# A two-layer graph network on one core: output addition one step later, 21 staged chunks, two early scatters for eighteen chunks, and 1 MB node transfers

## The chip, the cores and the metric

One core of one Trainium2 chip runs the whole program. The metric is the device time of one execution in microseconds (us); the median of three executions is compared. TensorE is called PE here, its weight loads PEld, VectorE DVE, ScalarE ACT, GpSimd POOL, and SyncE SP. SP issues nearly all plain DMA transfers, POOL all indirect ones (a row of 512 bytes for each of 128 indices).

## The reference

100000 nodes with 128 features, 50000 edges sorted by destination. A layer of graph attention and a layer of continuous-filter convolution follow each other, each behind a layer norm and a ReLU and with a residual:

```python
h = relu(layernorm(x))
x = x + gat(h, W_l, b_l, W_r, b_r, att, bias, src, dst)   # 4 heads, a self loop on every node
h = relu(layernorm(x))
x = x + filters(h, edge_attr_20, edge_weight, dst, src, W_in2f, Wf1, bf1, Wf2, bf2, Wo1, bo1, Wo2, bo2)

# gat:      m = leaky_relu(x_l[s] + x_r[d]);  e = m . att;  alpha = softmax of e over the edges of a destination
#           out[d] = sum of alpha * x_l[s] + bias
# filters:  msg = (h @ W_in2f)[src] * Wij(edge_attr) * edge_weight;  agg[dst] = sum of msg
#           out = ssp(agg @ Wo1 + bo1) @ Wo2 + bo2          # ssp(z) = softplus(z) - log 2
```

Here the convolution gathers at `idx_j = dst` and sums at `idx_i = src`.

## The kernel before

The work runs in four stages, one after the other on the same core. Nodes are handled in 49 groups of 2048 rows (1 MB), edges in 98 chunks of 512 (4 tiles of 128).

**Stage 1, dense nodes (to about 487 us).** A node with no edge attends only to itself, so its row is x + relu(norm(x)) W_l + bias. For each of the 49 groups SP loads x into one of four buffers `d_x` (`load`, L359) and stores the result from one of two buffers `d_x1` (`store`, L380), each in four transfers of 256 KB, a quarter of every partition's 8 KB row at a time (2 KB). The load of group g+4 is issued right behind the store of group g. DVE makes the statistics (`sums_d`, L877) and adds the residual in quarters (`x1_d`, L885); ACT normalises; PE transposes and multiplies (`step_d` on each engine). Beside the first four groups DVE prepares weights and edge lists (`beside`, L932) and PE turns the lists (`turn_lists`, `turn_last_list`). Meanwhile POOL gathers edge rows ahead (list `ahead`, L687): 18 **staged** chunks, which it writes on to DRAM (`store_stage`, L679) because there are only 24 slots for chunks, and then the first 18 chunks, which stay. Each entry of the list waits until a number of quarters of groups is done (`done`, L690).

**Stage 2, attention (to about 1434 us).** Fully unrolled over 98 chunks plus a lag: in step t the front of chunk t (scores) and the back of chunk c = t - 12 (shares, scan, output) run on the engines, in an order written out by hand (`step_a` on each engine). DVE's step is: difference `a_dif` (L1048); after ACT has copied the values, `a_u` (L1061); gate, product and scan of chunk c (L1067 to L1075); statistics of chunk t+4 (`sums_a`); in even steps the shift of a norm (`shifts`, L772), for which ACT waits before it normalises `a_ns` (L1294) and then makes `a_us` (L1347) and `a_xs` (L1349); then the output addition of chunk c into `a_xo` (L1096), which waits for PE's transposed product of the same step (L1609, `out_turned`); in odd steps the variances. Every seven chunks a pack of small row operations lies between. Once `a_xo` is there, SP stores the chunk (L447) and POOL writes its first tile of result rows into the node array (`early_scatters`, L659; the other three tiles wait for stage 3). POOL gathers the remaining 56 chunks, spread over the first 80 steps (L706 to L713); SP loads a staged chunk back when its slot is free (L451). In step t SP first issues the loads of shares and gates for chunk t - 11 (L439, L440), then waits for the addition of chunk t - 13 and stores it.

**Stage 3, convolution (to about 2637 us).** Chunks run in reverse order (97 first), so that a running sum carries over chunk borders. For each chunk POOL writes the three late tiles of the attention result (`scatters`, L718, L724) and adds the 4 tiles of messages of two chunks before into the sums in DRAM (`adds`, L728, L736); before the first add it waits until the additions of the previous chunk have landed.

**Stage 4, output network (to the end).** Over the 49 groups: load sums, load x1, compute, store, all in transfers of 1 MB with 8 KB a partition.

Of the kernel before, what the change touches and what calls it, by code (L numbers as in the profile page):

```python
# [34 lines left out]
TILES = 4  # L35
# [21 lines left out]
STAGED = 18  # L57
# [15 lines left out]
def gnn(nc, x, src, dst, edge_attr, edge_weight, W_l, b_l, W_r, b_r, att, bias,  # L73
# [27 lines left out]
    with ExitStack() as ctx:  # L101
# [239 lines left out]
        def late(s):  # L341

            return 16 * (TILES - EARLY[1 - s])
# [10 lines left out]
        def _(sp):  # L354
# [35 lines left out]
            for g in range(ROUNDS * RX, NG):  # L390
                if g == NG - 1:

                    sp.wait_ge(x1_stored[(g - 1) % RN], 16 * QUADS * in_slot[(g - 1) % RN])
                store(g, g % RX)
                if g + RX < NG:
                    load(g + RX, g % RX)
# [66 lines left out]
            for i in range(RN):  # L463
                sp.wait_ge(x1_stored[i], 16 * QUADS * in_slot[i])
                sp.sem_inc(sync_step, 1)
# [7 lines left out]
            for s in range(2):  # L473
                sp.wait_ge(end_stored[s], 16 * HALF)
                sp.wait_ge(early_scattered[s], 16 * EARLY[s] * HALF)
# [3 lines left out]
            def load_rows_b(k, u, t0):  # L479
# [12 lines left out]
                if t0 >= 2:  # L492
                    sp.wait_ge(x1_scattered[s], late(s) * turn(k, u - 2))
                    sp.sem_inc(sync_step, 1)
# [7 lines left out]
            def step_b(k, u, t0, ahead=True):  # L502
# [3 lines left out]
                if ahead:  # L506
                    load_rows_b(k, u + 1, t0 + 1)
# [11 lines left out]
            load_rows_b(0, 0, 0)  # L519
            for u in range(4):  # L520
                step_b(0, u, u)
            with sp.Fori(2, HALF - 1) as k:
# [6 lines left out]
            for s in range(2):  # L529
                sp.wait_ge(x1_scattered[s], late(s) * HALF)  # L530
# [38 lines left out]
        def _(pool):  # L569
# [89 lines left out]
            def early_scatters(t):  # L659
                s = t % 2  # L660
                pool.wait_ge(x1_ready, t + 1)
                if t >= 2:
                    pool.wait_ge(early_scattered[s], 16 * EARLY[s] * (t // 2))
                pool.sem_inc(pool_step, 1)
                for j in range(EARLY[s]):
# [23 lines left out]
            for n, (gather, t, h) in enumerate(ahead):  # L689
                done = QUADS * (RX + 1) + n * QUADS * (NG - RX - 3) // len(ahead)  # L690
# [5 lines left out]
            for i in range(RN):  # L696
                pool.wait_ge(x1_stored[i], 16 * QUADS * in_slot[i])
# [20 lines left out]
            def scatters(k, u):  # L718
# [4 lines left out]
                for j in range(EARLY[1 - s], TILES):  # L723
# [15 lines left out]
            for u in range(4):  # L739
                scatters(0, u)  # L740
                if u >= 2:
                    adds(0, u - 2, first=u == 2)
            with pool.Fori(2, HALF) as k:
                for u in range(2):
                    scatters(k, u)
# [32 lines left out]
        def _(dve):  # L778
# [98 lines left out]
            def sums_d(g, slot, m, half):  # L877
                if half == 0:
                    dve.wait_ge(xd_loaded[slot], 16 * QUADS * (m + 1))
# [5 lines left out]
            def x1_d(g, slot, m, q):  # L885

                dve.wait_ge(d_mm, QUADS * g + q + 1)
                if q == 0 and not (isinstance(g, int) and g < RN):
                    dve.wait_ge(x1_stored[slot % RN], 16 * QUADS * (RX // RN * m + slot // RN))
# [42 lines left out]
            beside = (output_bias, edge_lists, edge_weights, index_columns)  # L932
# [103 lines left out]
            def step_a(t):  # L1036
# [26 lines left out]
                if back:  # L1063
                    s = c % 2
                    dve.wait_ge(spread[s], 64 * (c // 2 + 1))
                    dve.wait_ge(keep_loaded[s], 16 * (c // 2 + 1))
                    dve.scalar_tensor_tensor(out=a_gate[:, :], in0=a_beta[s][:, :], scalar=-1.0, in1=a_keep[s][:, :],  # L1067
# [3 lines left out]
                    if c >= 1:  # L1071
                        dve.wait_ge(sum_scan, c)
# [18 lines left out]
                if back:  # L1091
                    dve.wait_ge(out_turned, c + 1)
                    if c >= 4:
                        dve.wait_ge(end_stored[s], 16 * ((c - 4) // 2 + 1))
                        dve.wait_ge(early_scattered[s], 16 * EARLY[s] * ((c - 4) // 2 + 1))
                    dve.tensor_tensor(a_xo[c % 4][:, :], bank[6 + c % 2][:, :], a_xd[c % DEPTH][:, :], ALU.add).then_inc(x1_ready, 1)  # L1096
# [9 lines left out]
            for i in range(RN):  # L1106
                dve.wait_ge(x1_stored[i], 16 * QUADS * in_slot[i])
            for t in range(NC + LAG):
# [3 lines left out]
            for s in range(2):  # L1112
                dve.wait_ge(end_stored[s], 16 * HALF)
                dve.wait_ge(early_scattered[s], 16 * EARLY[s] * HALF)
# [142 lines left out]
        def _(act):  # L1257
# [112 lines left out]
            for i in range(RN):  # L1370
                act.wait_ge(x1_stored[i], 16 * QUADS * in_slot[i])
# [16 lines left out]
            def norms_b(k, u, t0):  # L1388
# [4 lines left out]
                if t0 >= 2:  # L1393
                    act.wait_ge(x1_scattered[s], late(s) * turn(k, u - 2))
# [9 lines left out]
            def step_b(k, u, t0, ahead=True, front=True, mid=True, back=True):  # L1404
# [30 lines left out]
                if ahead:  # L1435
                    norms_b(k, u + 1, t0 + 1)
# [3 lines left out]
            norms_b(0, 0, 0)  # L1440
            for u in range(4):
                step_b(0, u, u, mid=u >= 1, back=u >= 2)
            with act.Fori(2, HALF - 1) as k:
# [34 lines left out]
        def _(pe):  # L1478
# [59 lines left out]
            for g in range(RX):  # L1538
                step_d(g, g, back=g > 0)
                if g == 0:  # L1540
                    output_bias()
                if g == 2:
                    turn_lists()
            turn_last_list()
# [199 lines left out]
```

## Time and profile before

| what | us |
|---|---|
| median of 3 runs (lowest, highest) | 3022.98 (3020.04, 3025.41) |
| the profiled execution, its own time | 3014.57 |
| its span, first to last instruction | 3012.7 |
| PE, DVE, ACT, POOL busy | 2392.7, 2267.1, 1939.7, 1908.9 |

The profiled execution is 8.4 us below the median of the other runs. A window row gives the busy time of each engine in a stretch, with the number of instructions in brackets, the granted TensorE clock, the busy share of the 16 DMA engines and the GB/s that they moved. A timeline row is one instruction (or a few of one kind merged) with its start and length in us; in brackets at its end stands how long its engine was idle before it and what ended that. A row of waits gives a line, what released it, the total of the idle time in us, how often, and the longest. "issue" is idle time in which the engine waited for nothing that the profile shows.

### The profile page before, as it was taken

The page shows a single profiled execution, that of the slowest core. Times are in us where ns is not written, and L with a number is a line of the kernel's source. Part 1 is how long each engine was busy: PE and PEld are TensorE (multiplying, and loading weights), DVE is VectorE, ACT ScalarE, POOL GpSimd, SP SyncE. Part 2 cuts the span into 40 slices and gives each one's busy share as a digit, 9 for nine tenths or more (in the row PEclk, how much of TensorE's full clock was granted, in tenths as well). Part 3 has the DMA queues.
Part 4 walks back from the last instruction along what each step waited for, and adds up shares of the span by engine and source line. Part 5 has one row for each costly group of instructions (what it writes and reads, how often), then busy time and mean ns, then how long its engine had stood idle before and what let it go on. Part 6 is the DMA issues. An engine that isn't in the chain of part 4 may idle for free. (4 is left out here: it accounts for less than half of the span.)

```text
span 3012.7 us, 59625 instructions
## 1 busy us (share of the span) xinstructions
PE 2392.7 (79%) x16506; PEld 1659.0 (55%) x16506; DVE 2267.1 (75%) x6293; ACT 1939.7 (64%) x4383; POOL 1908.9 (63%) x1650
## 2 busy tenths in 40 slices
PE   5888997998899998997677777777777777488777
PEld 4666664344444444445555555555555555377777
DVE  7777875688888878876787777777787787366666
ACT  5878886766666666660555555555555555289887
POOL 2677776377777777742588888888888888600000
PEclk9999998999999999996899899999899899789998
DMA  7999995266566655554566666666655656689998
GB/s 224 299 310 326 287 292 189 84 192 188 179 211 191 192 189 188 179 171 130 113 117 119 111 117 113 119 113 117 119 112 115 124 113 123 173 322 425 426 426 338
DMA packets 390076, 593.04 MB, mean 197 GB/s; under 512 B 148151, under 2 KB 225323, under 8 KB 364818
## 3 DMA queue, kind: packets, MB, share of 16 engines
q1 hardware_dynamic: 291682, 479.21, 48.4%
q0 software_dynamic: 98288, 112.65, 19.0%
q8 instruction: 39, 0.64, 0.1%
q14 instruction: 67, 0.55, 0.1%
HBM read 353.86 MB, written 246.47 MB: 199 GB/s over the span
## 5 line engine op out<-in xcount | busy, mean ns | idle before, releaser
L736 POOL DMA_INDIRECT sum_dram<-b_sum,b_at x392 | 636.9, 1625 | 148.5 <-issue 119.4
L650 POOL DMA_INDIRECT a_xs<-in_x,index x320 | 331.5, 1036 | 108.1 <-issue 98.9
L657 POOL DMA_INDIRECT a_xd<-in_x,index x320 | 328.7, 1027 | 97.5 <-issue 87.5
L724 POOL DMA_INDIRECT x_dram<-b_xo,sidx x294 | 312.7, 1064 | 105.1 <-issue 90.6
L1666 PE MATMUL bank<-b_rows,b_same 128*128 128x128 bf16 x4704 | 307.5, 231 | 0.6 <-ACT b_sum L1434 0.6
L1666 PEld LDWEIGHTS bank<-b_rows,b_same 128*128 128x128 bf16 x4704 | 292.6, 104 | 0.6 <-issue 0.6
L1275 ACT ACTIVATE d_n<-d_x,stat_d_shift,stat_d_rstd 128x128 f32<-128x128 f32 x686 | 283.5, 486 | 0.2 <-DVE stat_d_shift L772 0.2
L1699 PE MATMUL bank<-wo,f_ssp_out 128*128 128x128 f32 x1568 | 228.1, 292 | 63.1 <-DVE f_ssp_out L1221 61.5
L1699 PEld LDWEIGHTS bank<-wo,f_ssp_out 128*128 128x128 f32 x1568 | 204.4, 203 | 80.1 <-DVE f_ssp_out L1221 73.8
L1481 PE MATMUL bank<-ident,d_n 128*128 128x128 f32 x1184 | 193.2, 289 | 67.3 <-DMA d_n<-sum_dram 38.0
L1527 PE MATMUL bank<-wl,turned 128*128 128x128 f32 x1568 | 234.9, 295 | 10.8 <-ACT turned L1272 9.5
L1527 PEld LDWEIGHTS bank<-wl,turned 128*128 128x128 f32 x1568 | 196.8, 197 | 58.9 <-issue 35.7
L881 DVE BATCH_NORM_STATS2 stat_d_six<-d_x 128x6 f32<-128x128 f32 x784 | 160.4, 278 | 79.2 <-DMA d_x<-in_x 79.2
L666 POOL DMA_INDIRECT x_dram<-a_xo,index x98 | 117.6, 1200 | 155.6 <-DVE a_xo L1096 131.2
L1646 PEld LDWEIGHTS bank<-wo,b_msg 128*128 128x128 f32 x784 | 116.5, 226 | 169.5 <-issue 90.7
L1646 PE MATMUL bank<-wo,b_msg 128*128 128x128 f32 x784 | 134.1, 324 | 81.2 <-DVE b_msg L1162 80.8
L1061 DVE SCALAR_TENSOR_TENSOR a_u<-bank,cols,a_xs 128x512 f32<-128x512 f32 x98 | 73.6, 751 | 160.7 <-ACT a_xs L1349 160.7
L1235 DVE TENSOR_TENSOR d_x<-bank,d_x 128x512 f32<-128x512 f32 x180 | 123.0, 685 | 89.4 <-DMA out<-d_x 87.9
L1481 PEld LDWEIGHTS bank<-ident,d_n 128*128 128x128 f32 x1184 | 142.8, 148 | 84.7 <-DMA d_n<-sum_dram 38.1
L1294 ACT ACTIVATE a_ns<-a_xs,stat_e_shift,stat_e_rstd 128x128 f32<-128x128 f32 x392 | 160.7, 480 | 43.5 <-DVE stat_e_shift L772 43.5
L1424 ACT ACTIVATE b_rows<-bank 128x512 bf16<-128x512 f32 x98 | 58.4, 595 | 201.0 <-PE bank L1646 200.8
L1221 DVE SCALAR_TENSOR_TENSOR f_ssp_out<-bank,cols,f_ln_out 128x512 f32<-128x512 f32 x196 | 146.3, 746 | 53.8 <-ACT f_ln_out L1466 53.4
(234 smaller groups left out, 6138.8 us busy)
## 6 DMA issues: line engine op xcount, KB each, us to landing
d_x<-in_x SPq DMA_DIRECT2D x196, 256.0 KB
x_dram<-d_x SPq DMA_DIRECT2D x196, 256.0 KB
out<-d_x SPq DMA_DIRECT2D x49, 1024.0 KB, 10.1
sum_dram<-zero SPq DMA_DIRECT2D x48, 1024.0 KB
d_x<-x_dram SPq DMA_DIRECT2D x45, 1024.0 KB, 14.2
d_n<-sum_dram SPq DMA_DIRECT2D x25, 1024.0 KB, 11.9
a_beta<-beta_dram SPq DMA_DIRECT2D x392, 64.0 KB
x_end_dram<-a_xo SPq DMA_DIRECT2D x98, 256.0 KB, 3.0
```

Of the source, the lines that this page charges most:

```text
L650: pool.indirect_dma_start(a_xs[t % DEPTH][:, j * F:(j + 1) * F], None, x, column(t, j)).then_inc(gathered[t % GSEM], 16)
L657: pool.indirect_dma_start(a_xd[t % DEPTH][:, j * F:(j + 1) * F], None, x, column(t, TILES + j)).then_inc(gathered[t % GSEM], 16)
L724: pool.indirect_dma_start(x1_dram, bass.IndirectOffsetOnAxis(ap=sidx[s][:, j:j + 1], axis=0), b_xo[s][:, j * F:(j + 1) * F], None, bounds_ ...
L736: pool.indirect_dma_start(sum_dram, bass.IndirectOffsetOnAxis(ap=b_at[s][:, j:j + 1], axis=0), b_sum[s][:, j * F:(j + 1) * F], None, compu ...
L881: last = dve.bn_stats(stat_d[slot % 2]["six"][:, j, :], d_x[slot][:, j * F:(j + 1) * F])
L1275: last = act.activation(d_n[slot % RN][:, j * F:(j + 1) * F], d_x[slot][:, j * F:(j + 1) * F], ACT.Relu, scale=stat_d[slot % 2]["rstd"][:, ...
L1294: return act.activation(to[:, j * F:(j + 1) * F], rows[:, j * F:(j + 1) * F], ACT.Relu, scale=st["rstd"][:, n:n + 1], bias=st["shift"][:, ...
L1481: last = pe.transpose(to[0:width, j * P:(j + 1) * P], tiles[:, j * width:(j + 1) * width], ident[:, :])
L1527: last = pe.matmul(to[:, j * F:(j + 1) * F], turned[q % 2][:, j * P:(j + 1) * P], wl[:, :], start=False, stop=(j == 3))
L1646: last = pe.matmul(bank[5][:, j * F:(j + 1) * F], b_msg[:, j * P:(j + 1) * P], wo1[:, :], start=True, stop=True)
L1666: last = pe.matmul(bank[6][:, i * F:(i + 1) * F], b_same[s][:, j, i * P:(i + 1) * P], b_rows[s][:, part, j * F:(j + 1) * F], start=(j == 0 ...
L1699: last = pe.matmul(bank[4 + q][:, j * F:(j + 1) * F], f_ssp_out[q][:, j * P:(j + 1) * P], wo2[:, :], start=True, stop=True)
```

## The change

1. In stage 2 the output addition of chunk c moves from the end of DVE's step c + 12 into the next step, behind that step's scan and ahead of the statistics and the shift; there is one more step at the end. The gate's wait for the scan before moves ahead by two instructions.
2. 21 instead of 18 chunks are staged. The gathers ahead in stage 1 begin after group 3 instead of group 5; for that the index columns are made in the third group and the weights in the fourth, and PE turns the lists one group earlier.
3. For the last 18 chunks (80 to 97) two tiles instead of one are scattered early in stage 2, and two instead of three in stage 3, where these chunks come first. The loops of stage 3 on SP, ACT and POOL are split in two for it.
4. Each load and store of a node group in stage 1 is one transfer of 1 MB instead of four of 256 KB.

```diff
-STAGED = 18
+STAGED = 21
+LAST = 18
+RUNS = 1
+LAST_EARLY = 2
...
+        def early_of(c):
+            return LAST_EARLY if c >= NC - LAST else EARLY[c % 2]
...
             def load(g, slot):
-                for q in range(QUADS):
-                    sp.dma_start(d_x[slot][:, q * 512:(q + 1) * 512], node_rows(x, g)[:, q * 512:(q + 1) * 512]).then_inc(xd_loaded[slot], 16)
+                sp.dma_start(d_x[slot][:, :], node_rows(x, g)).then_inc(xd_loaded[slot], 16)
...
             def store(g, slot):
                 sp.wait_ge(d_x1_ready, QUADS * g + QUADS)
-                for q in range(QUADS):
-                    sp.dma_start(node_rows(x1_dram, g)[:, q * 512:(q + 1) * 512],
-                                 d_x1[slot % RN][:, q * 512:(q + 1) * 512]).then_inc(x1_stored[slot % RN], 16)
+                sp.dma_start(node_rows(x1_dram, g), d_x1[slot % RN][:, :]).then_inc(x1_stored[slot % RN], 16)
...
-                for j in range(EARLY[s]):
+                for j in range(early_of(t)):
                     pool.indirect_dma_start(x1_dram, column(t, 2 * TILES + j), a_xo[t % 4][:, j * F:(j + 1) * F], None,
...
-                done = QUADS * (RX + 1) + n * QUADS * (NG - RX - 3) // len(ahead)
+                done = QUADS * (RX - 1) + n * QUADS * (NG - RX - 1) // len(ahead)
...
-                for j in range(EARLY[1 - s], TILES):
+                for j in range(EARLY[1 - s] if later else LAST_EARLY, TILES):
                     pool.indirect_dma_start(x1_dram, bass.IndirectOffsetOnAxis(ap=sidx[s][:, j:j + 1], axis=0),
...
-            beside = (output_bias, edge_lists, edge_weights, index_columns)
+            beside = (output_bias, edge_lists, index_columns, edge_weights)
...
+                    if c >= 1:
+                        dve.wait_ge(sum_scan, c)
                     dve.scalar_tensor_tensor(out=a_gate[:, :], in0=a_beta[s][:, :], scalar=-1.0, in1=a_keep[s][:, :],
...
                     dve.tensor_tensor_scan(a_o[s][:, :], a_gate[:, :], a_pv[:, :], a_o[1 - s][:, C - 1:C] if c else 0.0,
                                            ALU.mult, ALU.add).then_inc(sum_scan, 1)
+                c = t - LAG - 1
+                if 0 <= c < NC:
+                    s = c % 2
+                    dve.wait_ge(out_turned, c + 1)
+                    if c >= 4:
+                        dve.wait_ge(end_stored[s], 16 * ((c - 4) // 2 + 1))
+                        dve.wait_ge(early_scattered[s], 16 * early_upto(c - 4))
+                    dve.tensor_tensor(a_xo[c % 4][:, :], bank[6 + s][:, :], a_xd[c % DEPTH][:, :], ALU.add).then_inc(x1_ready, 1)
...
-                if back:
-                    dve.wait_ge(out_turned, c + 1)
...
-                    dve.tensor_tensor(a_xo[c % 4][:, :], bank[6 + c % 2][:, :], a_xd[c % DEPTH][:, :], ALU.add).then_inc(x1_ready, 1)
...
-            for t in range(NC + LAG):
+            for t in range(NC + LAG + 1):
                 step_a(t)
```

## Rows read from the trace of the kernel before

**Rows 1.** Windows, three stages: length, busy by engine, clock, DMA share, GB/s

```profile
75.00:150.00 75.00, 66.66 (x438) 49.12 (x437) 58.32 (x233) 65.39 (x169) 49.80 (x55) 1.00 0.93 298
1700.00:1900.00 200.00, 143.83 (x1395) 112.99 (x1393) 154.73 (x414) 113.08 (x252) 161.50 (x118) 0.92 0.63 116
2700.00:2900.00 200.00, 159.50 (x1296) 152.70 (x1296) 137.97 (x215) 178.51 (x324) 0.00 (x0) 0.96 1.01 425
```

**Rows 2.** Waits of DVE, 80 to 470 us: line, releaser, total us, times, longest

```profile
DVE stat_d_six L881 <- DMA d_x<-in_x: 67.7, 37, 4.2
```

**Rows 3.** Timeline of DVE, first stage: start, us, engine, line, operation, idle before

```profile
82.28 0.18 DVE L772 SCALAR_TENSOR_TENSOR stat_d_shift<-stat_d_sum,stat_d_rstd 128x16 f32<-128x16 f32 x1 [0.30 <-ACT stat_d_rstd L768]
341.54 0.17 DVE L772 SCALAR_TENSOR_TENSOR stat_d_shift<-stat_d_sum,stat_d_rstd 128x16 f32<-128x16 f32 x1
349.78 0.18 DVE L772 SCALAR_TENSOR_TENSOR stat_d_shift<-stat_d_sum,stat_d_rstd 128x16 f32<-128x16 f32 x1
455.11 0.17 DVE L772 SCALAR_TENSOR_TENSOR stat_d_shift<-stat_d_sum,stat_d_rstd 128x16 f32<-128x16 f32 x1
```

**Rows 4.** Windows with 2 KB packets alone, and with gathers alone

```profile
65.00:85.00 20.00, 17.80 (x113) 13.83 (x113) 16.79 (x68) 17.75 (x46) 0.39 (x1) 0.91 0.70 218
505.00:540.00 35.00, 30.88 (x99) 11.71 (x98) 19.04 (x76) 26.45 (x66) 26.47 (x29) 1.00 0.18 54
```

**Rows 5.** POOL: first and last gather of stage 1, its longest wait after

```profile
84.61 1.05 POOL L675 DMA_INDIRECT a_xs<-in_x,index  x1 [39.36 <-issue]
472.70 0.94 POOL L657 DMA_INDIRECT a_xd<-in_x,index  x1 [0.30 <-issue]
POOL x_dram L666 <- DVE a_xo L1096: 41.6, 1, 41.6
```

**Rows 6.** Waits of ACT, 600 to 1280 us

```profile
ACT a_ns L1294 <- DVE stat_e_shift L772: 39.0, 37, 1.4
```

**Rows 7.** Timeline of odd steps of the second stage, DVE and ACT

```profile
603.23 0.67 ACT L1347 ACTIVATE a_us<-bank,cols 128x512 f32<-128x512 f32 x1
604.05 0.60 ACT L1349 ACTIVATE a_xs<-bank 128x512 f32<-128x512 f32 x1 [0.16 <-PE bank L1586]
1283.68 0.16 DVE L772 SCALAR_TENSOR_TENSOR stat_e_shift<-stat_e_sum,stat_e_rstd 128x16 f32<-128x16 f32 x1
1283.76 0.68 DVE L1096 TENSOR_TENSOR a_xo<-bank,a_xd 128x512 f32<-128x512 f32 x1
1283.87 1.65 ACT L1294 ACTIVATE a_ns<-a_xs,stat_e_shift,stat_e_rstd 128x128 f32<-128x128 f32 x4 [1.23 <-DVE stat_e_shift L772]
1285.74 0.69 ACT L1347 ACTIVATE a_us<-bank,cols 128x512 f32<-128x512 f32 x1 [0.22 <-PE bank L1584]
1286.60 0.60 ACT L1349 ACTIVATE a_xs<-bank 128x512 f32<-128x512 f32 x1 [0.17 <-PE bank L1586]
```

**Rows 8.** End of stage 2: a wait of DVE; timeline, SP and DVE

```profile
DVE a_xo L1096 <- PE bank L1609: 21.0, 14, 2.2
1392.96 0.42 SPq L440 DMA_DIRECT2D a_keep<-gate_dram  x1
1396.05 0.69 DVE L1067 SCALAR_TENSOR_TENSOR a_gate<-a_beta,a_keep 128x512 f32<-128x512 f32 x1 [1.23 <-DMA a_keep<-gate_dram]
```

**Rows 9.** Stage 3: groups of the page, waits of POOL, DVE timeline

```profile
L736 POOL DMA_INDIRECT sum_dram<-b_sum,b_at x392 | 636.9, 1625 | 148.5 <-issue 119.4
L724 POOL DMA_INDIRECT x_dram<-b_xo,sidx x294 | 312.7, 1064 | 105.1 <-issue 90.6
POOL sum_dram L736 <- DMA sum_dram<-b_sum,b_at: 10.1, 7, 1.8
POOL x_dram L724 <- DMA sum_dram<-b_sum,b_at: 6.1, 20, 0.3
1459.16 0.69 DVE L1126 TENSOR_TENSOR b_y<-b_x,bo_row 128x512 f32<-128x512 f32 x1
1468.30 0.69 DVE L1126 TENSOR_TENSOR b_y<-b_x,bo_row 128x512 f32<-128x512 f32 x1
```

More of the change, by code:

```diff
@@ L339, in early, with early_upto, scattered_b @@
             return EARLY[s] * F
-        def late(s):
-            return 16 * (TILES - EARLY[1 - s])
+        def early_of(c):
+            return LAST_EARLY if c >= NC - LAST else EARLY[c % 2]
+        def early_upto(c):
+            return sum(early_of(i) for i in range(c % 2, c + 1, 2))
+        def scattered_b(k, u, later):
+            s = u % 2
+            few = 16 * (TILES - LAST_EARLY)
+            many = 16 * (TILES - EARLY[1 - s])
+            if not later:
+                return few * turn(k, u)
+            return many * turn(k, u) - (many - few) * (LAST // 2)
         def node_rows(a, g):
@@ L492, in load_rows_b @@
                 if t0 >= 2:
-                    sp.wait_ge(x1_scattered[s], late(s) * turn(k, u - 2))
+                    sp.wait_ge(x1_scattered[s], scattered_b(k, u - 2, later))
                     sp.sem_inc(sync_step, 1)
@@ L517, in step_b @@
                 sp.dma_start(b_col[s][:, :], columns[:, bass.ds(8 * (NC - 1 - t), 8)]).then_inc(b_col_ld[s], 16)
-            load_rows_b(0, 0, 0)
+            load_rows_b(0, 0, 0, later=False)
             for u in range(4):
-                step_b(0, u, u)
-            with sp.Fori(2, HALF - 1) as k:
+                step_b(0, u, u, later=False)
+            with sp.Fori(2, LAST // 2) as k:
+                for u in range(2):
+                    step_b(k, u, 4 + u, later=False)
+            step_b(LAST // 2, 0, 4, later=False)
+            step_b(LAST // 2, 1, 5)
+            with sp.Fori(LAST // 2 + 1, HALF - 1) as k:
                 for u in range(2):
@@ L716, in _, with scatters @@
             pool.wait_ge(cleared, 16 * NG)
-            def scatters(k, u):
+            def scatters(k, u, later):
                 s = u % 2
@@ L739, in _ @@
             for u in range(4):
-                scatters(0, u)
+                scatters(0, u, False)
                 if u >= 2:
                     adds(0, u - 2, first=u == 2)
-            with pool.Fori(2, HALF) as k:
+            with pool.Fori(2, LAST // 2) as k:
                 for u in range(2):
-                    scatters(k, u)
+                    scatters(k, u, False)
+                    adds(k, u - 2)
+            with pool.Fori(LAST // 2, HALF) as k:
+                for u in range(2):
+                    scatters(k, u, True)
                     adds(k, u - 2)
@@ L1393, in norms_b @@
                 if t0 >= 2:
-                    act.wait_ge(x1_scattered[s], late(s) * turn(k, u - 2))
+                    act.wait_ge(x1_scattered[s], scattered_b(k, u - 2, later))
                 act.activation(b_xo[s][:, early(1 - s):], b_x[s][:, early(1 - s):], ACT.Copy).then_inc(b_xo_ready, 1)
@@ L1435, in step_b @@
                 if ahead:
-                    norms_b(k, u + 1, t0 + 1)
+                    norms_b(k, u + 1, t0 + 1, later)
             act.wait_ge(ones_set, 1)
             inverse_deviation(act, stat_e[0], TILES, b_var, b_logv, b_rstd, 1)
-            norms_b(0, 0, 0)
+            norms_b(0, 0, 0, later=False)
             for u in range(4):
-                step_b(0, u, u, mid=u >= 1, back=u >= 2)
-            with act.Fori(2, HALF - 1) as k:
+                step_b(0, u, u, mid=u >= 1, back=u >= 2, later=False)
+            with act.Fori(2, LAST // 2) as k:
+                for u in range(2):
+                    step_b(k, u, 4 + u, later=False)
+            step_b(LAST // 2, 0, 4, later=False)
+            step_b(LAST // 2, 1, 5)
+            with act.Fori(LAST // 2 + 1, HALF - 1) as k:
                 for u in range(2):
```

42 lines of the change are left out of this document (19 added, 23 removed).

## The prediction

> **What bounds the kernel now.** The four stages follow each other, so I read each by itself: first the windows, then the waits of each stage, then single steps in the timeline. The chain that ended last is of little use here: it begins at 2584 us and covers stage 4, which the change leaves alone.
>
> In stage 1 the DMA engines are busy for 0.93 of the time at 298 GB/s, while ACT and PE stand at 65 to 67 of 75 us [rows 1]. DVE waits 67.7 us in 37 of about 43 groups for the load of x [rows 2]. From one shift to the same shift of the next group is 8.24 us in an undisturbed pair; over 42 groups, 82.28 to 455.11, the mean is 8.88 us [rows 3]. So the engines could do 8.24 and the loads make it 8.88. Does that bandwidth explain it? Before the gathers start, 2 KB packets alone move 218 GB/s at a share of 0.70, so 311 GB/s at full share or 105 ns a packet and engine; gathers alone make 54 GB/s at 0.18, 300 GB/s or 27 ns for a row of 512 B [rows 4]. A group is 1024 packets of 2 KB (1024 x 0.105 / 16 = 6.72 us), its part of the 36 staged stores (36 x 128 x 0.105 / 16 / 42 = 0.72) and 288 / 42 = 6.9 gathers (6.9 x 128 x 0.027 / 16 = 1.49): 8.9 us, just the mean period. Stage 1 is bound by DMA.
>
> Stage 2 is a round trip between DVE, ACT and PE, read below in single steps. In stage 3 POOL is busy 161.5 of 200 us [rows 1], and with the gap of some 0.3 us behind every indirect transfer it is full: four adds at (636.9 + 148.5) / 392 = 2.0 us and three scatters at (312.7 + 105.1) / 294 = 1.4 us [rows 9] are 12.3 us a chunk, start of the stage included. Its other engines can do better: while POOL does not yet hold them, two chunks follow each other in 9.14 us [rows 9].
>
> **1 MB transfers (stage 1).** The bytes stay; 256 packets of 8 KB replace 1024 of 2 KB in a group, and SP issues one DMA where it issued four. No row shows 8 KB packets in stage 1; the nearest is stage 4, which moves 1 MB transfers at 425 GB/s and share 1.01 [rows 1], 311 ns for 8 KB. A group's 256 packets then take 256 x 0.311 / 16 = 4.98 us instead of 6.72. The staged stores and gathers of the change (42 and 312) add 0.84 + 1.5. The sum is 7.3 us, under 8.24: ACT's chain becomes the bound, and 42 x (8.88 - 8.24) = **27 us** fall away. The bounds are 7.3 us (nothing left to wait for) and the present price of a byte, 6.72 + 2.34 = 9.06 us, which would cost 42 x 0.18 = 8 us. I take the row of stage 4, because its transfers have the very shape; the two prices meet the 8.24 us at 5.9 us for 2 MB, 355 GB/s. Nothing waits for a quarter today (every wait counts all four), so larger transfers hold nobody up.
>
> The Trainium skill (DMA: Bandwidth & Descriptors, "Why small descriptors are slow (HBM only)") speaks against this: a packet costs its 32-byte beats and about three cycles more. By that, 64 + 3 against 256 + 3 beats, bytes would get only 3.4% cheaper, the group would take 8.8 us, and stage 1 would gain some 3 us. The rows at 311 and 425 GB/s say 27% instead, though of different stages; it stays a rival.
>
> **Three more staged chunks.** 24 gathers and 6 stores move from stage 2 into stage 1. There POOL is busy from 84.61 to 473.6 [rows 5], about 1.25 us a gather without a pause; it grows by 24 x 1.25 + 6 x 0.6 = 34 us and begins some 17 us sooner (two groups), so it ends near 490, after the dense groups, which then end near 455. That costs nothing: POOL goes straight on to its six resident chunks (48 x 1.25 = 60 us; today it has to wait for the last stores first), is through some 6 us later than now, and now waits 41.6 us there for the first addition of stage 2 [rows 5]. That addition comes 27 us sooner by stage 1 and 8 us later by its own step: 41.6 - 6 - 27 + 8 = 17 us of slack are left. In stage 2, 24 gathers less help nobody: DVE never waits there for a gather. If that cover were gone, each chunk late by x would cost x.
>
> **The addition one step later (stage 2).** DVE has the same instructions in every step, and in steady steps it did not wait for PE's product, because the statistics lay between. Moving the addition saves nothing there. But in even steps it passes the shift: scan, addition, statistics, shift. The shift comes an addition later, 0.68 less the 0.08 by which neighbours overlap, 0.60 us, while the next `a_dif` stays in place. ACT already waits for that shift 39.0 us in 37 steps [rows 6], and then runs `a_ns` 1.65, `a_us`, `a_xs`, for which DVE's `a_u` waits. The slack is 0.22 + 0.17 us in a plain odd step and 0.16 in one with pack work [rows 7], so `a_xs` is late by 0.21 or 0.44. Of the 40 odd steps from 15 to 93, 23 are in pack phases 1 to 4: 23 x 0.44 + 17 x 0.21 = **+13.7 us**. Bounds: 0, were PE late anyway, and 40 x 0.60 = 24.
>
> At the end, where statistics run out, DVE does wait for PE: 21.0 us in 14 steps [rows 8]. This goes, but not in full. SP is moved too: it now waits for an addition that comes after the next chunk's scan before it issues the next loads of shares and gates. From that addition to a usable gate are about 0.5 us for the store, 1.75 for four loads and 3.1 for the gate (issued 1392.96, used 1396.05 [rows 8]), 5.4 us, and then gate, product, scan and addition, 3.2 us: 8.6 us for two steps, 4.3 a step, against 4.5 to 5.4 now. Followed chunk by chunk the tail ends **6.5 us** sooner; bounds 0 and 14. POOL's second early scatter behind the last chunk adds **1.3 us**. The other 17 fall into waits of POOL and are covered. Stage 2: +8.5 us in sum.
>
> **Two early scatters (stage 3).** 18 scatters of 1.4 us leave POOL, but the first three chunks fill the pipeline and POOL idles there; 15 count. The new wait: adds of a chunk wait until the last adds have landed, today hidden behind three scatters. In 20 chunks the landing fell into the gap just before a scatter, in 7 it came after all three and cost 1.4 us each [rows 9]. So it usually takes two to four us, three scatters cover 4.1, two cover 2.7. I take 0.4 us of new wait, 1.36 - 0.4 = 0.96 for each of 15, **14 us** gained. Bounds: 0.35 each (all land late, 5 us) and 1.36 (20 us). The other engines' 9.14 us stay below POOL's 11.
>
> **Sum.** -27 + 13.7 - 6.5 + 1.3 - 14 = -33 us. Against the profiled execution's own 3014.6 that is 2982; against the median of 3022.98, 8.4 us higher, **2990 us**.
>
> **The rivals.** (a) *A byte keeps its price in stage 1.* Then stage 1 runs at 8.8 to 9.06 us a group, -3 to +8 us, by the rule above or by plain queueing of loads and stores. For it: the two prices come from different stages. Against it: stage 4 is also full of mixed loads and stores. With the rest (+8.5 - 14) it gives 3014 to 3026. (b) *Slower*, the same mechanism with the new wait of stage 3 at its bound: the extra gathers and stores make stage 1 DMA-bound at 9.06 (+8), the late shift costs 13.7 - 5, and the adds land late (-5): 3023 + 8 + 8.7 - 5 = 3035. It decides where 2 MB take more than 6.6 us beside the gathers. (c) *The late shift costs the full 0.60* in every odd step and the tail gains nothing, because PE's turning and SP's loads hold it: +24 instead of +7, 3007. (d) *POOL sets the pace*, so that fewer gathers speed up stage 2: its gaps there are all near 0.3 us, and 24 x 1.25 = 30 us more would go, 2960. Against it: DVE waits for ACT, not for gathers. (e) *The change does not do what it says*, the shorter first stage being eaten by POOL's longer list: 2990 + 27 = 3017.
>
> **How the numbers follow.** Forecast 0.66; (a) 0.11; (b) 0.06; (c) 0.09; (d) 0.04; (e) 0.04. The forecast's own range is 2972 to 3004, from its bounds. The range 2965 to 3014 takes in (c) and the near end of (a). What a measurement can tell from no change is about 0.2%, 6 us. Faster: forecast, (c), (d), a part of (e) and half of (a), 0.86; same: the rest of (a) and (e), 0.07; slower: (b) and what little of (c) costs more, 0.07.
>
> **What would show it.** Right: a period of 8.2 to 8.3 us in stage 1, hardly any wait for x, and a DMA share near 0.85 there; ACT's wait for the shift up by 20 to 25 us; the tail's steps at 4.3 us with DVE waiting for gates instead of PE; POOL in the first 18 chunks of stage 3 at 10.5 to 11 us with short waits on the adds. Wrong: a share still at 0.93 and periods of 8.8; an unchanged wait for the shift; a stage 2 that shrinks by more than 10 us; scatters and adds at 12 us a chunk from the first on.

## The result, and the profile after

The changed kernel takes **2997.46 us** in the median of its runs (2997.24 to 2999.34), against 3022.98 before: a ratio of 0.9924, 95% interval 0.9902 to 0.9946, or 25.5 us less (16 to 30 by the interval). The forecast was 2990 us with a range of 2965 to 3014. The profiled execution took 2997.2 us (span 2995.3), 17.4 us less span than the profiled execution of before; that one happened to be 8 us under its own median, so the traces account for 17 of the 25 us.

Reading the same instructions in both timelines divides these 17.4 us: the first difference of stage 2 (`a_dif` of chunk 0) starts at 456.6 instead of 492.2 (-35.6); the way from there to the last addition takes 964.2 instead of 937.5 us (+26.7); from there to the first add of stage 3 nothing changes; stage 3 from its first add to the start of the last four is 1149.7 instead of 1161.8 (-12.0); the rest +3.6, which is scatter (below). So stage 1 gave more than forecast, and stage 2 took most of it away.

The windows of after (length, busy time by engine, clock, DMA share, GB/s), stages 1 and 4, to be read against [rows 1]:

```profile
75.00:150.00 75.00, 71.28 (x469) 52.83 (x468) 63.05 (x254) 69.51 (x181) 58.58 (x66) 1.00 0.96 340
150.00:225.00 75.00, 71.81 (x471) 53.13 (x471) 63.79 (x256) 70.05 (x182) 59.06 (x67) 1.00 0.97 350
...
2700.00:2900.00 200.00, 158.55 (x1288) 151.53 (x1287) 139.52 (x216) 178.53 (x323) 0.00 (x0) 0.96 1.01 426
```

In stage 1 PE and ACT are now busy 71 and 70 of 75 us, and DMA moves 340 to 350 GB/s. But its share did not fall to 0.85: it is still 0.96 to 0.97. The waits of DVE in stage 1 (80 to 455 us), against [rows 2]:

```profile
DVE d_x L911 <- PE bank L1555: 25.4, 52, 1.4
DVE stat_d_shift L793 <- ACT stat_d_rstd L789: 24.9, 38, 0.7
DVE stat_d_six L902 <- DMA d_x<-in_x: 7.9, 14, 1.5
```

The wait for x fell from 67.7 us to 7.9. In its place DVE waits for PE and ACT, so the engines set the pace. Two shifts 41 periods apart, against [rows 3]:

```profile
79.47 0.18 DVE L793 SCALAR_TENSOR_TENSOR stat_d_shift<-stat_d_sum,stat_d_rstd 128x16 f32<-128x16 f32 x1 [0.20 <-ACT stat_d_rstd L789]
419.50 0.18 DVE L793 SCALAR_TENSOR_TENSOR stat_d_shift<-stat_d_sum,stat_d_rstd 128x16 f32<-128x16 f32 x1 [0.74 <-ACT stat_d_rstd L789]
```

(419.50 - 79.47) / 41 = 8.29 us a group: ACT's 8.24 with little on top.

Stage 2: the waits of ACT from 600 to 1280 us, against [rows 6]; the wait of DVE for gathered rows near the end of the stage (1160 to 1305 us); and its wait for gates in the tail (1344 to 1425 us):

```profile
ACT a_ns L1317 <- DVE stat_e_shift L793: 51.8, 37, 3.2
...
DVE stat_e_six L978 <- DMA a_xd<-in_x,index: 11.1, 3, 8.2
...
DVE a_gate L1090 <- DMA a_keep<-gate_dram: 17.9, 5, 5.4
```

The first line is the late shift (39.0 us before): 12.8 us more, where the prediction looked for 20 to 25. Also behind the addition now is the row work of the packs on DVE, for which ACT waits 54.1 us in this stretch (rows `p_dec`, `p_run`, `p_exp`, `p_col`), 29.0 before. The third shows the tail as forecast in kind: DVE waits for SP's loads, where it waited for PE ([rows 8]). The second is something that the prediction does not have. Before, DVE waited 0.3 us in all for gathers near the end of the stage; now one step of 9.5 us becomes one of 17.9. The timeline of DVE and POOL around that step:

```profile
1285.71 0.67 DVE L1105 TENSOR_TENSOR a_xo<-bank,a_xd 128x512 f32<-128x512 f32 x1
1286.29 0.66 DVE L996 TENSOR_REDUCE p_col<-p_tail 32x1 f32<-32x513 f32 x1
1295.15 0.87 DVE L978 BATCH_NORM_STATS2 stat_e_six<-a_xs 128x6 f32<-128x128 f32 x4 [8.20 <-DMA a_xd<-in_x,index]
...
1260.22 1.01 POOL L683 DMA_INDIRECT x_dram<-a_xo,index  x1 [3.77 <-DVE a_xo L1105]
...
1287.32 1.02 POOL L683 DMA_INDIRECT x_dram<-a_xo,index  x1 [0.77 <-issue]
1288.64 0.97 POOL L674 DMA_INDIRECT a_xd<-in_x,index  x1 [0.30 <-issue]
1289.92 0.95 POOL L674 DMA_INDIRECT a_xd<-in_x,index  x1 [0.31 <-issue]
```

DVE has nothing to do from 1286.95 to 1295.15. The two gathers of `a_xd` at 1288.64 and 1289.92, whose rows then land, stand in POOL's order behind the early scatter at 1287.32. That scatter sends the sum of the addition that is now a step later; at 1260.22 POOL stood still 3.77 us for another such addition, with all later gathers behind it. POOL's list spreads the gathers over the scatters of the first 80 chunks, not over the first 80 steps; the scatter at 1287.32 is that of chunk 78, which DVE adds in step 91 now, the long step, and added in step 90 before. POOL's waits for additions, from 700 us to the last gathers, before (to 1323 us) and after (to 1306 us):

```profile
POOL x_dram L666 <- DVE a_xo L1096: 1.1, 1, 1.1
...
POOL x_dram L683 <- DVE a_xo L1105: 47.8, 14, 10.0
```

So POOL is not short of time in the changed kernel, which has 24 gathers fewer here: before, it ran behind the additions and hardly ever waited for one; now it stands still for 47.8 us, with gathers that DVE will need behind the wait.

Stage 3: the groups of the page (busy us, mean ns, idle before), against [rows 9]:

```profile
L753 POOL DMA_INDIRECT sum_dram<-b_sum,b_at x392 | 639.6, 1632 | 155.0 <-issue 108.7
L741 POOL DMA_INDIRECT x_dram<-b_xo,sidx x276 | 292.7, 1060 | 102.3 <-issue 87.4
```

and POOL's wait for the adds to land in the first sixteen chunks (1460 to 1640 us):

```profile
POOL sum_dram L753 <- DMA sum_dram<-b_sum,b_at: 12.7, 10, 1.7
```

Eighteen scatters have left L741. The sixteen periods from the first add of a chunk to that of the next take 11.3 us in the mean, 12.0 before (forecast: 10.5 to 11); further on both kernels have 11.96.

### The profile page after: what moved, and what is told of

Same layout as the page of the kernel before. It is cut to its first block, busy times and chain, and to the rows that moved or that the text cites. A ratio compares the mean times of both kernels' runs of the same rounds, so it can differ in the third digit from the quotient of the medians.

```text
span 2995.3 us, 58792 instructions
## 1 busy us (share of the span) xinstructions
PE 2392.2 (80%) x16506; PEld 1653.3 (55%) x16506; DVE 2264.1 (76%) x6293; ACT 1932.7 (65%) x4383; POOL 1903.8 (64%) x1656
## 4 chain that ended last, share of the span: by engine, by line
DMA 18%; issue 9%; POOL 8%; DVE 6%; PE 4%; SPq 3%; ACT 2%; POOLq 0%; DVEq 0%; ACTq 0%
DMA out<-d_x 7%; POOL sum_dram L753 5%; DMA b_end<-ends 4%; DMA sum_dram<-b_sum,b_at 3%; POOL x_dram L741 3%; DMA x_dram<-b_xo,sidx 2%; PE bank L1695 2%; DVE d_x L1258 1%; DMA b_w<-weight_dram 1%; DVE stat_e_six L1152 1%; DVE f_ssp_out L1244 1%; PE bank L1675 1%; DVE b_y L1149 1%; ACT f_exp_out L1488 1%; DVE b_s L1190 1%
## 5 line engine op out<-in xcount | busy, mean ns | idle before, releaser
L674 POOL DMA_INDIRECT a_xd<-in_x,index x308 | 316.7, 1028 | 93.9 <-issue 92.6
L667 POOL DMA_INDIRECT a_xs<-in_x,index x308 | 312.4, 1014 | 93.9 <-issue 91.7
L741 POOL DMA_INDIRECT x_dram<-b_xo,sidx x276 | 292.7, 1060 | 102.3 <-issue 87.4
L683 POOL DMA_INDIRECT x_dram<-a_xo,index x116 | 134.7, 1162 | 165.0 <-DVE a_xo L1105 125.4
L1174 DVE TENSOR_TENSOR_SCAN b_fill<-b_goes,b_fill,bank 128x512 f32<-128x512 bf16 x97 | 124.0, 1278 | 76.3 <-DMA b_goes<-goes_dram 75.7
L1483 ACT ACTIVATE f_abs_out<-bank,cols 128x512 f32<-128x512 f32 x196 | 136.9, 698 | 60.3 <-PE bank L1509 59.9
## 6 DMA issues: line engine op xcount, KB each, us to landing
d_x<-x_dram SPq DMA_DIRECT2D x45, 1024.0 KB, 14.2
```

Of the source, the lines that this page charges most:

```text
L667: pool.indirect_dma_start(a_xs[t % DEPTH][:, j * F:(j + 1) * F], None, x, column(t, j)).then_inc(gathered[t % GSEM], 16)
L674: pool.indirect_dma_start(a_xd[t % DEPTH][:, j * F:(j + 1) * F], None, x, column(t, TILES + j)).then_inc(gathered[t % GSEM], 16)
L741: pool.indirect_dma_start(x1_dram, bass.IndirectOffsetOnAxis(ap=sidx[s][:, j:j + 1], axis=0), b_xo[s][:, j * F:(j + 1) * F], None, bounds_ ...
```

## The experiments

All were timed beside the kernel before. Ratios are to that kernel; the changed one stands at 0.9924. This table gives stretches of each profiled execution in us, read as above: start of `a_dif` of chunk 0; from there to that of chunk 84; on to that of chunk 97, the last; on to the last addition (the tail); on to the first add of stage 3; its first 16 chunks; the others to the start of the last four adds; and to the end.

```
kernel             first a_dif  to 84  to 97  tail  to add  16 ch.  others  end
before                   492.2  745.5  118.4  73.7    36.9   192.3   969.4  384.4
after                    456.6  755.2  132.3  76.7    36.8   180.8   969.0  388.0
e1 add_back              460.1  746.9  118.1  75.1    38.6   181.9   973.4  380.5
e2 gathers_sooner        456.7  755.9  119.2  73.5    37.6   180.6   968.7  382.8
e3 quarters              491.9  755.6  132.6  74.1    38.3   182.4   967.5  384.2
e4 one_early             459.1  755.7  132.3  73.9    37.7   190.0   971.0  381.0
e5 staged18              456.8  757.9  126.2  74.1    39.5   182.1   970.9  384.9
e6 behind_shift          457.4  852.0  134.4  75.0    38.3   182.3   972.1  387.2
e7 behind_store          456.6  857.2  137.7  62.0    37.7   181.8   974.8  381.2
e8 last30                457.1  858.4  137.3  62.7    39.8   181.2   962.3  383.5
e9 hybrid                457.4  748.2  117.7  62.9    39.1   183.1   971.8  382.1
e10 hybrid_last30        457.1  746.1  132.7  63.9    40.1   178.8   965.5  380.7
e11 hybrid_staged18      456.0  744.8  119.6  63.6    39.4   181.2   965.8  380.4
e12 only_1mb             460.9  747.1  123.0  74.9    38.0   191.5   968.3  391.0
```

The last column has the same instructions in all kernels and lies between 380.4 and 391.0: the 3.6 us above are of that kind.

**e1: the addition back in its place.** The block goes back behind the shift, with the chunk of its own step (`c = t - LAG`):

```diff
-                c = t - LAG - 1
-                if 0 <= c < NC:
...
                     shifts(dve, stat_e[pair % 2], 4 * TILES, rstd, shift, pair + 1)
+                if back:
+                    dve.wait_ge(out_turned, c + 1)
...
-            for t in range(NC + LAG + 1):
+            for t in range(NC + LAG):
```

> The changed kernel with the addition back behind the shift of its own step; transfers, staged chunks and scatters stay changed. Theory: the later addition cost stage 2 all that it lost, 9.8 us up to step 84 (the shift that comes after it in even steps), 13.9 us in steps 85 to 92 (the gathers that POOL issues behind the scatter of this addition come a step later, and DVE waits for them) and 3 us in the tail. Undone, the time is 2997 - 24 = 2973 us (2967 to 2982), ACT's wait for the shift is back near 39 us, and no step near the end of the stage is 18 us long. Rival: stage 2 lost its time to the gathers that the three staged chunks and the shorter stage 1 pushed into it; then the long steps 85 to 92 stay, only the 9.8 us come back, and the time is 2985 to 2990 us. Rival two: the tail needs the later addition; then the tail takes 6 us more and the time is 2979 to 2983.

Measured: 2974.75 us, 0.9845 (0.9825 to 0.9865): 0.8% or 24 us faster than with the later addition. ACT's wait for the shift, 600 to 1280 us, is that of before:

```profile
ACT a_ns L1315 <- DVE stat_e_shift L793: 38.5, 37, 1.4
```

The steps up to 84 take 8.3 us less, those from 84 to 97 14.2. The late addition alone made stage 2 slower, and without it the change gives twice as much. The long steps that the first rival would have kept are gone: step 91 takes 9.6 us.

**e2: gathers a step sooner.** Addition as in the changed kernel; in POOL's loop:

```diff
-                until = min(len(rest), -(-len(rest) * (t + 1) // (NC - LAG - 6)))
+                until = min(len(rest), -(-len(rest) * (t + 2) // (NC - LAG - 6)))
```

> The changed kernel, but POOL issues behind the scatter of chunk t the gathers that stood behind that of chunk t+1, so that the gathers come when they came before the change. Theory: the 13.9 us lost in steps 85 to 92 are waits of DVE for gathers that stand in POOL's order behind the scatter of an addition that comes a step later; with the gathers a step sooner the wait of DVE for a_xd near the end (11.1 us in 3 steps) is gone, the time is 2997 - 13 = 2984 us (2980 to 2988), and the wait for the shift stays at 47 us. Rival: POOL is full there, so the gathers cannot come sooner; the wait stays and the time is 2995 to 2999. Rival two: the sooner gathers wait for buffers that are not free and hold up the scatters behind them; slower, 3000 to 3010.

Measured: 2981.39 us, 0.9877 (0.9855 to 0.9900). The waits of DVE from 1160 to 1290 us hold no gathers any more:

```profile
DVE a_u L1082 <- ACT a_xs L1372: 20.9, 13, 2.3
DVE a_u L1082 <- issue: 2.5, 1, 2.5
```

The stretch from 84 to 97 falls from 132.3 to 119.2; the tail is 3.2 us shorter, and all else up to the last adds stays within 1 us. POOL had room; the gathers merely stood behind the wrong scatter.

**e3: the node rows in quarters again.**

```diff
-                sp.dma_start(d_x[slot][:, :], node_rows(x, g)).then_inc(xd_loaded[slot], 16)
+                for q in range(RUNS):
+                    sp.dma_start(d_x[slot][:, q * 512:(q + 1) * 512], node_rows(x, g)[:, q * 512:(q + 1) * 512]).then_inc(xd_loaded[slot], 16)
```

and the stores in the same way, with `RUNS = 4`.

> The changed kernel with the node rows of stage 1 in four transfers of 256 KB again, loads and stores both. Theory: 2 KB packets cost more time for a byte than 8 KB packets in this stage too; the period goes from 8.3 back to 8.9 to 9.1 us, DVE waits 60 us or more for x again, and the time is 2997 + 30 = 3027 us (3021 to 3036). Rival: stage 1 became shorter because the gathers start some 20 us sooner and are spread otherwise, not by the size of the transfers; then the period stays at 8.3 to 8.5 and the time at 2997 to 3004.

Measured: 3031.26 us, 1.0043 (1.0028 to 1.0058), 1.2% or 36 us more than the changed kernel. Its groups take 9.0 us in the mean. A window of stage 1:

```profile
150.00:225.00 75.00, 66.64 (x435) 48.92 (x435) 56.79 (x228) 65.96 (x169) 58.79 (x67) 1.00 0.98 326
```

and DVE's wait for x (80 to 455 us):

```profile
DVE stat_d_six L905 <- DMA d_x<-in_x: 66.8, 37, 4.4
```

The wait is back (66.8 us), and so is the first `a_dif` at 491.9. At nearly the same share the DMA engines move 326 GB/s here and 350 in the changed kernel, of the same mix of rows, staged stores and gathers.

**e12: 1 MB transfers alone**, put into the kernel before (the edit of e3 the other way round).

> The kernel before with nothing but the 1 MB transfers of the node rows in stage 1, loads and stores. Theory: they alone bring the period from 9.0 to 8.3 us and end stage 1 some 34 us sooner; stage 2 has no later addition, so all of it stays: 3023 - 34 = 2989 us, 0.989 (0.9865 to 0.9905). Rival: a part of the shorter stage 1 came from the gathers' earlier start (20 us sooner); then the gathers end later, stage 2 waits for the first ones, and the gain is 20 us or less: 0.9935 to 0.996.

Measured: 2994.12 us, 0.9910 (0.9892 to 0.9928), just beyond the first range (0.9905), which lies in the interval. The first `a_dif` comes at 460.9, 31 us sooner than before and 4 later than in the changed kernel; the steps from 84 to 97 take 4.6 us more than before, for which DVE waits 3.4 us for gathers. So the transfers do nearly all of stage 1; alone they are worth as much as the whole change.

**e4: one early scatter.** `LAST_EARLY = 1`, loops still split.

> The changed kernel with one early scatter in the last eighteen chunks, as in all others; the loops of stage 3 stay split. Theory: the eighteen scatters go back to stage 3, where POOL is full; sixteen chunks there take 12.0 us instead of 11.3, stage 3 is 11.5 us longer, stage 2 ends 1 us sooner at most, and the time is 2997 + 11 = 3008 us (3004 to 3013). Rival: with two early scatters the tail of stage 2 is held up by POOL as much as stage 3 gains; then 2997 to 3002. Rival two: the wait for the landing of the adds costs less than it seems; then 2997 + 18 = 3015.

Measured: 3002.65 us, 0.9949 (0.9931 to 0.9967), 7.5 us more than the changed kernel; the intervals overlap. The trace is plainer: 190.0 instead of 180.8 us for sixteen chunks, and a tail (73.9) like that of e2 with two (73.5). POOL's wait for the adds to land there (1469 to 1660 us):

```profile
POOL sum_dram L753 <- DMA sum_dram<-b_sum,b_at: 0.7, 1, 0.7
```

against 12.7 us in 10 with two early scatters: the new wait exists, and it eats a part of what the scatter saves. The 9.2 us of the traces lie between the theory (11) and the first rival (none); its held-up tail is not seen.

**e5: 18 staged chunks.** `STAGED = 18`.

> The changed kernel with 18 staged chunks instead of 21; POOL gathers 24 rows' columns more in stage 2. Against the kernel before, the changed kernel stands at 0.9924. Theory: POOL has room in stage 2 (it waits 73 us there for additions), so the staged chunks bring nothing; stage 1 gives the same 8.3 us period, the stretch to step 84 stays at 755 us, the long steps 85 to 92 stay or grow by 1 to 3 us: 0.992 to 0.994. Rival: the three chunks are what gives POOL its room; without them the gathers are late in the whole stage and the time is 15 to 30 us more, 0.997 to 1.002. Rival two: stage 1 is eased by 24 gathers and 6 stores less, -5 us, 0.9905.

Measured: 2993.68 us, 0.9906 (0.9885 to 0.9927), within the uncertainty of the changed kernel. The ratio is that of the second rival, but not by its way: stage 1 is the same to 0.2 us. The late gathers still cost DVE, a little less than with 21 (126.2 us from step 84 to 97, not 132.3), and why less stays open; e11 repeats this without them.

**e6: the addition a step later, but behind the shift**, with the gathers of e2. The block of `a_xo` moves from behind the scan:

```diff
-                c = t - LAG - 1
-                if 0 <= c < NC:
...
                     shifts(dve, stat_e[pair % 2], 4 * TILES, rstd, shift, pair + 1)
+                c = t - LAG - 1
+                if 0 <= c < NC:
```

> The changed kernel with the gathers a step sooner, and with the addition still a step later than before, but behind the shift in its step instead of ahead of it. Theory: the 9.8 us lost up to step 84 are the late shift; with the addition behind it they come back in full, ACT's wait for the shift is near 39 us again, the tail is that of the later addition, and the time is 9 us under that of the kernel with sooner gathers alone (0.9877 of the kernel before): 0.9847. Rival: the 9.8 us are the price of a fuller step of DVE, not of the shift; then nothing changes, 0.9877. Rival two: additions later in the step make scatters, and the gathers behind them, later again; steps near the end grow and the time is 0.988 to 0.992.

Measured: 3100.61 us, 1.0248 (1.0224 to 1.0271), some 125 us more than the theory gave, by something that none of the three theories had. A wait of PE from 600 to 1200 us:

```profile
PE bank L1604 <- DVE a_xo L1119: 99.3, 56, 3.7
```

and two rows of the timeline:

```profile
717.40 0.67 DVE L1119 TENSOR_TENSOR a_xo<-bank,a_xd 128x512 f32<-128x512 f32 x1
718.13 0.39 PE L1604 MATMUL bank<-bias_d,ones 3*128 3x512 bf16 x1 [1.64 <-DVE a_xo L1119]
```

PE opens each step with the base of a chunk's output (L1604), in one of two banks, and waits for the addition that empties it. With the addition a step later, this is the one that DVE makes in the step just gone; at the end of that step it comes too late, and PE's whole next step, behind which ACT and DVE wait, starts after it. In e2, with the addition right behind the scan, PE's waits in the same stretch don't contain it. So of the two places that were tried for the later addition, early in the step makes the shift pay, and late makes PE pay. The 9.8 us of the theory can't be read from this run.

**e7 and e8: on top of e6.** e7 lets SP store a sum a step later, so that its loads don't stand behind that wait; e8 alone has two early scatters in the last 30 chunks as well.

```diff
-                c = t - LAG - 1
+                c = t - LAG - 2
...
-LAST = 18
+LAST = 30
```

> As the kernel with the addition behind the shift and sooner gathers, and SP waits for an addition, to store it, a step later than there, so the loads of shares and gates no longer stand behind that wait. Theory: in the tail the gates' loads set the pace of 4.6 us a chunk; with them issued earlier the seven chunks behind the last shares go at 3.3 to 3.6 us, the tail is 66 to 68 us instead of 73.5, and the time is 6 us under its sister: 0.9827. Rival: the loads also wait until the product of two chunks earlier has left their buffer, and the tail stays within 1 us: 0.9847. Rival two: the later store of a chunk's rows holds up the additions four chunks on; slower by 3 to 8 us, 0.986 to 0.987.

> As the kernel with the later store, and two early scatters in the last thirty chunks instead of eighteen. Theory: twelve more chunks of stage 3 go at 11.3 us instead of 12.0, 8.4 us less, and the twelve scatters of 1.3 us fall into waits of POOL in stage 2, which has some 60 us of them: 8 us under its sister, 0.980. Rival: POOL is full where these chunks are gathered (steps 80 to 92), the gathers come late again and eat 8 us or more: 0.9827 to 0.987.

Measured: 3087.33 us, 1.0209 (1.0186 to 1.0232), and 3080.73 us, 1.0190 (1.0166 to 1.0213). Both inherit PE's wait. Against e6 the tail of e7 is 62.0 instead of 75.0 us: the loads did set its pace. Against e7, e8 gains 12.5 us in the later chunks of stage 3, 8.6 of them in the twelve that the edit changes (136.2 us instead of 144.8; forecast 8.4); the rest is scatter, and its ratio is not separable.

**e9: each place where it is cheap.** The old place up to step 93, none in step 94, then a step later behind the scan; SP's store as in e7. The first block stands behind the scan, the second, for `c = t - LAG`, behind the shift:

```diff
+                c = t - LAG - 1
+                if t > NC - LEAD and 0 <= c < NC:
...
+                if back and t < NC - LEAD:
```

> The changed kernel with the addition in its old place, behind the shift of its own step, up to step 93, none in step 94, and from step 95 a step later, right behind the scan; SP waits for an addition, to store it, a step later than now. Theory: the steady steps cost what they did before the change (747 us to step 84, 82 us from there to 93), PE finds its bank free, and the tail, where DVE waited for PE, gets the later addition with gates loaded earlier: 66 to 69 us instead of 75.1 in the kernel with the addition back. Against the kernel before, that kernel stood at 0.9845; this one 7 us lower: 0.982. Rival: the tail is set by the shares of the last pack, 33 us behind the last difference, and by the way from there; then the tail is within 2 us of 75 and the ratio is 0.984 to 0.985. Rival two: the switch costs a bank, PE waits for the addition in steps 95 to 97 and the tail grows: 0.986.

Measured: **2964.12 us, 0.9811** (0.9789 to 0.9833), faster than the kernel before and the changed one. The steps cost what they did before, and the tail is 62.9 us. DVE's wait for gates in it (1323 to 1386 us) went from 17.9 us to

```profile
DVE a_gate L1090 <- DMA a_keep<-gate_dram: 5.2, 4, 3.5
```

SP's later store without the later addition was not run. In the tail of e1 (1325 to 1401 us) DVE waits 1.3 us for gates and 21.1 us for PE's product, so there the loads have little to give: it takes both edits.

**e10: e9 with two early scatters in thirty chunks.**

> The hybrid kernel (addition in its old place up to step 93, later in the tail, SP's store a step later), and two early scatters in the last thirty chunks instead of eighteen. Theory: twelve more chunks of stage 3 at 11.3 instead of 12.0 us, their scatters fall into waits of POOL in stage 2 (57 us with the addition back): 8 us under its sister, 0.9795. Rival: POOL's order delays the gathers again near steps 80 to 92, and half or more is lost: 0.981 to 0.985.

Measured: 2966.91 us, 0.9826 (0.9806 to 0.9847): no gain over e9. Stage 3 is 10.6 us shorter (9.4 in the twelve chunks that the edit changes), and steps 84 to 97 are 15.0 us longer, by the wait that the changed kernel has (DVE, 1160 to 1305 us):

```profile
DVE stat_e_six L978 <- DMA a_xd<-in_x,index: 12.8, 3, 7.0
```

Here the addition is in its old place; twelve scatters more, some 1.3 us each, ahead of the last gathers suffice. POOL's order near the end of stage 2 has hardly any slack, whatever uses it up.

**e11: e9 with 18 staged chunks.**

> The hybrid kernel with two early scatters in the last eighteen chunks, and 18 staged chunks instead of 21. Without the late gathers of the changed kernel in the way, this shows what the three staged chunks are worth. Theory: nothing; POOL has the room for 24 gathers more in stage 2, stage 1 stays at 8.3 us a group because ACT sets it, steps up to 84 take 748 us and those from 84 to 93 take 82: 0.981, within 0.002. Rival: POOL becomes too full with 30 us of gathers more, DVE waits for them near steps 84 to 93, and 5 to 15 us are lost: 0.983 to 0.986. Rival two: stage 1 starts sooner or runs faster with fewer gathers: 0.9795 or less.

Measured: 2961.65 us, 0.9815 (0.9800 to 0.9829), the same as e9: three more staged chunks are worth nothing that can be measured.

## Why the prediction was right, and where its steps failed

**Stage 1 (forecast -27, measured -35.6; e3 gives 36).** The mechanism was right: loads too slow by packet size, ACT next in line (PE is as busy, but waits for ACT's `d_n` 13.5 us in 40, and ACT for PE 4.2 us in 6, 80 to 455 us). Two sizes were off. First a counting error: the shifts at 82.28 and 455.11 [rows 3] are 41 periods apart, not 42, so the mean was 9.09 us, not 8.88; 41 x (9.09 - 8.29) = 33 us, and the shorter first groups add the other 3. Second, the price of a packet: 311 ns for 8 KB was the price of stage 4, and a group was to need 7.3 us (7.4, as 312 gathers come to 1.6 us by the same formula, not 1.5). The trace has 340 / 0.96 = 354 and 350 / 0.97 = 361 GB/s at full share, where e3 has 326 / 0.98 = 333: the mix got 6 to 8% cheaper, not 18%. A group then needs 0.97 x 8.29 = 8.0 us, only just under ACT's 8.24. That the size came out so well is luck in part, because ACT's floor cut the gain off; had ACT been faster, the forecast would have been too good by 0.7 us a group. With 2.3 us a group for staged stores and gathers as in the working, an estimate, the rows alone went from 0.98 x 9.0 - 2.3 = 6.5 us in e3 to 8.0 - 2.3 = 5.7, 12% less, where stage 4's row had 26%. The estimate from the Trainium skill's overhead per packet (DMA: Bandwidth & Descriptors, "Why small descriptors are slow (HBM only)"), 3.4%, is too low here.

**Three more staged chunks (forecast nothing).** Right by e11 and, within its uncertainty, e5.

**The late shift (forecast +13.7).** Right in kind and nearly in size: +9.7 us to step 84 between the two traces, and 8.3 between e1 and after. The odd steps grew by some 0.46 us with pack work (0.44 forecast) and 0.13 without (0.21 forecast), and a few even steps became up to 0.8 us shorter. The row work of the packs, which comes later too, is not the cause: even steps with it (phases 0 to 2 of a pack's seven steps) keep their length to 0.1 us, and the odd steps of phase 4, which have none behind the addition, grow by 0.47 like those of phases 1 and 2. The sign was too large (ACT's wait 12.8 us up, not 20 to 25).

**The gathers behind the scatter (not in the forecast, +13.9).** This is the step that failed. The working counted what the later addition does to SP, and said of POOL only that its waits for additions are covered and that DVE never waits for a gather; "if that cover were gone, each chunk late by x would cost x". The cover was gone: POOL issues in order, the early scatter waits for the addition, and the last gathers stand behind it. Before, the slack there was under a step (0.3 us of waiting already, DVE, 1190 to 1330 us). e2 took these 13 us back by nothing but the order.

**The tail (forecast -6.5).** It is -1.6 at most (e2 against e1: 73.5 and 75.1), +3 in the changed kernel's own trace; e3 and e5, with the same code there, have 74.1, +0.4. The mechanism held: steps of two chunks, set by SP's loads (from the first gate behind the last shares to the last one 27.5 us for six in e2, 4.6 each, where 4.3 were forecast and 4.9 measured before). But the working let all steps of the tail gain. The first half ends with the shares of the last pack, 33 us after the last `a_dif` with either place (32.8 in e1, 33.5 in e2), so the later addition gains nothing up to there; and the last addition needs one step more. Only with the loads taken out from behind SP's wait (e9) does the tail give 12 us, 2 of them up to those shares (31.0) and the rest behind them, at 3.5 us a step. The second early scatter (+1.3) shows nowhere: 36.9 and 36.8 us to the first add.

**Two early scatters (forecast -14).** 11.5 us by the two traces, 9 by e4. The new wait was mis-sized a little: 12.7 us in 10 less the usual 0.3 each are 9.7, 0.6 us for each of 16 chunks, not 0.4.

In sum, -33 was forecast, the traces give -17.4 and the medians -25.5. Stage 1 gave 8.6 us more than forecast, which made up for half of what stage 2 cost more (26.7 against 8.5); that two misses of opposite sign met is luck, and the total is closer than its terms; the rest is stage 3 and the scatter of the last stage. Of the rivals, (c) came nearest for stage 2 (+24), but by another cause.

## What to carry to other kernels

When an instruction is moved, list every in-order queue that waits for its result, and read what stands behind that wait on each, at the stage's end too, where slack is smallest: here a gather behind a scatter, loads behind a store and a bank of PE each decided more than the instruction itself. Take a move apart by regime: the later addition costs in the steady steps, and having it in the tail alone, with SP's loads set free (e9), is 33 us faster than having it everywhere. A gain that is cut off by the next engine's floor hides a wrong price; check the price itself, by GB/s over share, before using it elsewhere.

## What the runs showed of the hardware that was not expected

1 MB transfers of 8 KB packets move 426 GB/s at a share of 1.01 in stage 4, but with staged stores and gathers beside them in stage 1 340 to 350 at 0.96 to 0.97; 2 KB packets there 316 to 326 at 0.96 to 0.98. So a share near one does not say that the engines move all they can, and a price from one mix does not carry to another. The adds of stage 3 land late enough that, with two scatters in between instead of three, POOL waits 0.9 to 1.7 us for them in ten of sixteen chunks.
